# Reciprocal deviations of the tokens spread over channels through DRAM instead of by matmuls

## The reference, cut to what matters

```python
mu = jnp.mean(xs, axis=-1, keepdims=True)
var = jnp.mean((xs - mu) ** 2, axis=-1, keepdims=True)
xn = (xs - mu) / jnp.sqrt(var + EPS) * ln_g + ln_b
mid = jax.nn.silu(xn @ fc1_w + fc1_b) @ fc2_w + fc2_b
qkv = (xs @ qkv_w)...          # q, k normed by head, linear attention, o normed
o = o + mid
o = o @ proj_w + proj_b
```

## Time and profile before

| | |
|---|---|
| median of 3 runs | 2871.93 us (2860.03 to 2872.58) |
| the profiled execution's own time | 2866.76 us |
| its span | 2864.9 us |
| PE busy | 2757.2 us, 96% of the span |
| PE weight loads busy | 2522.9 us |
| DVE busy | 2035.1 us, 71% |
| ACT busy | 1184.9 us, 41% |
| POOL busy | 687.1 us, 24% |
| mean granted PE clock | 0.964 of full |

### The profile page before, as it was taken

One profiled execution on the slowest core, in us unless ns is written; L12 is line 12 of the kernel. 1 busy time (PEld: TensorE's weight loads), 2 busy tenths in 40 slices (PEclk: granted clock), 3 DMA queues, 4 the chain that ended last, 5 costly groups with the idle time before them and its releaser, 6 DMA issues.

```text
span 2864.9 us, 41194 instructions
## 1 busy us (share of the span) xinstructions
PE 2757.2 (96%) x14894; PEld 2522.9 (88%) x14894; DVE 2035.1 (71%) x2635; ACT 1184.9 (41%) x2043; POOL 687.1 (24%) x211
## 2 busy tenths in 40 slices
PE   6997799999999999999999999999999999999999
PEld 4555699899998899899998899999999899999998
DVE  5968784988887694988887693888887634444443
ACT  3431365444432366444442265444442254333332
POOL 0010052222224053322224053322224033211220
PEclk9998799999999999999999999999999999999999
DMA  5247642333236732333236733233326732111110
GB/s 218 61 120 236 218 126 76 96 96 96 97 117 212 254 123 89 96 96 96 96 104 212 264 115 99 76 107 100 102 96 196 270 97 68 39 39 47 41 39 30
DMA packets 189739, 341.14 MB, mean 119 GB/s; under 512 B 10720, under 2 KB 173152, under 8 KB 186720
## 3 DMA queue, kind: packets, MB, share of 16 engines
q1 hardware_dynamic: 180528, 311.59, 33.4%
q0 software_dynamic: 4480, 19.27, 2.3%
q10 hardware_dynamic: 4528, 7.57, 0.8%
HBM read 234.89 MB, written 103.51 MB: 118 GB/s over the span
## 4 chain that ended last, share of the span: by engine, by line
PE 77%; issue 9%; DVE 5%; DMA 5%; ACT 2%; POOL 1%; SPq 1%; DVEq 0%; ACTq 0%; POOLq 0%
PE bank L756 16%; PE bank L758 16%; PE bank L757 16%; PE bank L802 4%; PE bank L961 4%; PE bank L963 4%; PE bank L962 4%; PE bank L1161 3%; PE bank L983 3%; PE bank L1145 2%; DMA X<-x_scr 2%; DVE AC L2379 1%; PE bank L1112 1%; PE bank L1216 1%; PE bank L732 1%
## 5 line engine op out<-in xcount | busy, mean ns | idle before, releaser
L1728 ACT ACTIVATE S<-bank,b1p 128x448 f32<-128x448 f32 x336 | 212.8, 633 | 875.5 <-PE bank L758 873.8
L2379 DVE SCALAR_TENSOR_TENSOR AC<-XV,wfold,AC 128x1568 f32<-128x1568 f32 x288 | 530.4, 1847 | 2.8
L756 PE MATMUL bank<-SH,W2H 128*128 128x448 f32 x1008 | 393.2, 390 | 4.4 <-DVE SL L2348 4.4
L758 PE MATMUL bank<-SH,W2L 128*128 128x448 f32 x1008 | 377.9, 375 | 0.0
L757 PE MATMUL bank<-SL,W2H 128*128 128x448 f32 x1008 | 376.6, 374 | 0.0
L756 PE MATMUL bank<-XRH,W1H 128*128 128x448 f32 x1008 | 373.6, 371 | 0.0
L758 PE MATMUL bank<-XRH,W1L 128*128 128x448 f32 x1008 | 370.1, 367 | 0.0
L757 PE MATMUL bank<-XRL,W1H 128*128 128x448 f32 x1008 | 369.1, 366 | 0.0
L674 POOL TENSOR_TENSOR rq<-qn,nhalf 112x32 f32<-112x32 f32 x28 | 181.9, 6495 | 427.9 <-DVE qn L2318 427.9
L666 POOL TENSOR_TENSOR rk<-kn,nhalf 112x24 f32<-112x24 f32 (+1 forms) x56 | 200.8, 3598 | 285.8 <-DVE kn L2140 285.8
L678 POOL TENSOR_TENSOR ro<-on,nhalf 112x32 f32<-112x32 f32 x28 | 179.8, 6422 | 311.6 <-DVE on L2339 311.5
(11 more groups left out here) (237 smaller groups left out, 5375.4 us busy)
## 6 DMA issues: line engine op xcount, KB each, us to landing
X<-x_scr SPq DMA_DIRECT2D x52, 672.0 KB, 5.1
XV<-in_xp SPq DMA_DIRECT2D x36, 870.0 KB, 6.7
XC<-in_xp SPq DMA_DIRECT2D x14, 1682.0 KB, 11.9
CQ<-q_scr SPq DMA_DIRECT2D x28, 672.0 KB, 7.7
CX<-in_x SPq DMA_DIRECT2D x28, 672.0 KB, 4.9
x_scr<-CX SPq DMA_DIRECT2D x28, 672.0 KB, 5.7
V<-v_scr SPq DMA_DIRECT2D x28, 672.0 KB, 4.9
Y<-x_scr SPq DMA_DIRECT2D x28, 672.0 KB, 4.2
```

The lines of the kernel that those rows point to most:

```text
L756: mm(o, wh, xh, start=first, stop=False)
L758: return mm(o, wl, xh, start=False, stop=stop)
L1728: fn(S[:, j % 2, :], bank[j % 2][:, 0:T], ACT.Silu, bias=b1p[:, j:j + 1]).then_inc(s["s_s"], 1)
L2379: stt(o, XV[h][:, ky:ky + HR, kx:kx + W], wfold[:, kind, k, 3 * ky + kx:3 * ky + kx + 1], o, ALU.mult, ALU.add).then_inc(s["va"], 1)
```

## The change

The diagonal matrices, the 8 matmuls and the bank are taken out. ACT instead issues two DMAs for each tile: a write of rr (112 x 4) to a DRAM scratch of 448 numbers, and, once that write has landed, a read of these 448 numbers to each of the 128 partitions (RB). `scale_x` waits for the read and multiplies by RB. The waits of PE for `xsr`, and one for `oc_ev` ahead of the first tile's `spread_r`, go too.

```diff
@@ buffers
-        rh, rl = sb("rh", [TS, SUB], F32R, at=at), sb("rl", [TS, SUB], at=at)
-        DH, DL = sb("DH", [TS, SUB, TS], F32R, at=at), sb("DL", [TS, SUB, TS], F32R, at=at)
+        RB = sb("RB", [P, T], at=list(at))
+        at[0] += 2 * C * 4
-        o1r = sb("o1r", [TS, P], F32R, at=at)
+    r_d = scratch("r_scr", (SUB, TS))
@@ PE
-                def spread_r(n, p):
-
-                    pe.wait_ge(s["dg"], n * 2 + 2)
-                    for u in range(SUB):
-                        mm(bank[p][:, u * TS:(u + 1) * TS], o1r[:, :], DH[:, u, :], start=True, stop=False)
-                        last = mm(bank[p][:, u * TS:(u + 1) * TS], o1r[:, :], DL[:, u, :], start=False, stop=True)
-                    last.then_inc(s["rb_mm"], 1)
@@ PE, offset_dots
-                    pe.wait_ge(s["xsr"], n0 + 1)
@@ PE, last tile of the key and value stage
-                        if (t, u) == (STRIPS - 1, 3):
-                            if nxt:
-                                pe.wait_ge(s["oc_ev"], (b + 2) * (2 * KC))
-                            spread_r(n0, 7)
@@ PE, attend
-                    if u == 1:
-                        pe.wait_ge(s["xsr"], n + 1)
@@ PE, pre, step 4
                         pe.wait_ge(s["ml"], n * KC)
-                        spread_r(n, 6)
                         query_norms(n, 7)
@@ ACT
+                def roots_out(n):
+
+                    act.wait_ge(s["rr_s"], n + 1)
+                    act.dma_start(r_d.rearrange("u p -> p u"), rr[:, :], allow_slow_non_contiguous=True).then_inc(s["r_st"], 16)
+
+                def roots_spread(n):
+
+                    act.wait_ge(s["r_st"], n * 16 + 16)
+                    act.dma_start(RB[:, :], r_d.rearrange("(o u) p -> o (u p)", o=1).to_broadcast([P, T])).then_inc(s["r_ld"], 16)
@@ ACT, last tile of the key and value stage
+                        if (t, u) == (STRIPS - 1, 1):
+                            roots_out(n0)
                         values_out(n, t, u)
+                        if (t, u) == (STRIPS - 1, 2):
+                            roots_spread(n0)
@@ ACT, tile
                     silu(n, 6)
                     if not last:
+                        roots_out(n + 1)
                         query_out(n + 1, 1)
                         query_out(n + 1, 2)
+                        roots_spread(n + 1)
                     silu(n, 7)
@@ DVE (the call of token_diag is gone from both stages)
-            def token_diag(n):
...
-            def scale_x(n, p):
-                dve.wait_ge(s["rb_mm"], n + 1)
-                tt(X[:, :, :], X[:, :, :], bank[p][:, 0:T].unsqueeze(1).to_broadcast([P, KC, T]), ALU.mult).then_inc(s["xsr"], 1)
+            def scale_x(n):
+                dve.wait_ge(s["r_ld"], n * 16 + 16)
+                tt(X[:, :, :], X[:, :, :], RB[:, :].unsqueeze(1).to_broadcast([P, KC, T]), ALU.mult).then_inc(s["xsr"], 1)
```

More of the change, by code:

```diff
@@ L262, in build @@
             wo_ld kxs kxh kxl k_mm v_mm k_sq k_ev v_ev k_red k_rs k_hat v1_st0 v1_st1 at_mm ab_s
-            x_ld v_ld y_ld y_st xh xl xt_mm bn_s ag_s rve_s rr_s rh_s rl_s dg rb_mm xsr xrh xrl
+            x_ld v_ld y_ld y_st xh xl xt_mm bn_s ag_s rve_s rr_s r_st r_ld xsr xrh xrl
             q_mm q_ev qq qs_mm qn_s rq_s qa_mm o_sc o_mx o_sq o_red ro_s o_fin ot_mm
@@ L2218, in keys_values @@
                         key_scale(n - 1, 1 - t % 2, 1)
-                    if last:
-                        first_tile("diag")
                     if nxt:
@@ L2232, in keys_values @@
                             dve.wait_ge(s["ktp"], KTB + (b + 1) * (2 * KC))
-                        dve.memset(f(o1r[:, :]), 1.0)
                         for u in range(2):
@@ L2255, in run @@
                         token_var(n)
-                    elif what == "diag":
-                        token_diag(n)
                     elif what == "scale":
-                        scale_x(n, 7)
+                        scale_x(n)
                     elif what == "split":
@@ L2429, in tile @@
                     conv(t, 4)
-                    if not last:
-                        token_diag(n + 1)
                     split_s(n, 5)
@@ L2443, in tile @@
                     if not last:
-                        scale_x(n + 1, 6)
+                        scale_x(n + 1)
                         query_norm(n + 1, 7)
```

## The result

| | before | after |
|---|---|---|
| median | 2868.12 us (2858.72 to 2872.58, 6 runs) | 2842.23 us (2832.71 to 2849.12, 6 runs) |
| profiled execution, its own time | 2866.76 us | 2844.07 us |
| its span | 2864.9 us | 2842.3 us |
| mean granted PE clock | 0.964 | 0.966 |

The ratio is 0.9908, with a 95% interval from 0.9888 to 0.9928. The changed kernel is 25.9 us faster, where the forecast's terms gave 33.1 us (23.5 + 7.7 + 1.9).

What follows compares the result with a forecast made beforehand. PE, busy 96% of the span, was taken as the bound. 2866.76 - 23.5 (matmuls) - 7.7 (clock) - 1.9 (DVE) = 2833.7 us, plus 1 us towards the runs' mean: 2835 us, 8-in-10 range 2814 to 2858.

Steps and rivals of the forecast that it cites:

- The matmuls removed: Eight spread matmuls leave PE in each of 28 tiles, 0.84 us per tile, all on the path: -23.5 us.
- PE's clock: Less poorly filled time on PE around the norms: some 5 fewer clock falls of 1.54 us each, -7.7 us.
- the starting count: Before the change, 21 of 24 regular tiles' 8 us windows show a PE clock under 1.00, three show 1.00.
- DVE: DVE loses 1.48 us of work per tile; PE's waits for ML in images 0 to 2 go, -1.9 us.
- is worth nothing by itself: DVE's removed `token_diag` work, 41 us over 28 tiles, gains nothing by itself because DVE is not the bound.
- the rival of the taken gain: In images 0 to 2 PE's 0.84 us per regular tile goes to other waits, no clock gain: 2858 us, chance 0.10.
- The DMAs: ACT's write and read per tile, taken as 3 and 2 us, are covered by other work: 0 us.
- The cover of 5.6 us up to ACT and 6.7 us up to PE: Time from the write's issue to its landing beyond which ACT is late (5.6 us) and PE waits (6.7 us).
- the list of what would show me wrong: DVE or PE waiting for the DMA, the write landing after over 5 us, or falls moving the other way.
- The rival of the slow write: The 4-byte write lands late and holds ACT, then PE; at 10 us landing, 2913 us; chance 0.08.
- the estimate of 24 us for each us: Every us of write landing beyond PE's cover costs 24 us over the regular tiles.

Runs made afterwards that it cites:

- e12: Changed kernel, but DVE still does its four operations on the reciprocals, whose results nobody uses: 2846.31 us, ratio 0.9935.
- e2: Kernel before, with buffers rh and rl moved behind the others so that XRH, XRL and S lie 64 bytes lower: 2873.79 us, ratio 1.0016.
- e1: Changed kernel with 64 bytes left free behind rr, putting XRH and XRL back at their old addresses: 2837.39 us, ratio 0.9894.
- e3: Changed kernel with the scratch as 112 x 4, a contiguous write, and DVE reading RB with a stride: 2848.93 us, ratio 0.9928.
- e4: Changed kernel without its two DMAs, X multiplied by a constant -0.5 instead of the reciprocals: 2837.25 us, ratio 0.989.
- e5: Changed kernel with e1's padding and a contiguous write, PE turning every fourth token so RB is read as before: 2831.76 us, ratio 0.9876.
- e8: Changed kernel with RB read from 128 different rows of the input, reciprocals not applied: 2840.81 us, ratio 0.9909.
- e7: Changed kernel with only 8 of the 24 small query-norm matmuls per tile, so the norms are wrong: 2815.66 us, ratio 0.9822.
- e13: As e10, but the 24 norm matmuls stay together in the first tile of images 0 to 2: 2814.17 us, ratio 0.9830.
- e9: Changed kernel with the write issued and waited for twice: 3119.87 us, ratio 1.0883.
- e10: e5's kernel with the norm matmuls in two groups of 12, nine second-layer matmuls of block 6 between them: 2827.7 us, ratio 0.9853.

## Why the prediction was right, and where it was not

**The matmuls removed (-23.5 us): right.** The norms start 0.20 us after the W1L matmul. At equal time at the lower clock, a tile of the last image is 0.55 us shorter, and the other 0.29 us are in the W1 pitch. Over all runs, the clock-free time is 14.9 us lower, and the terms for matmuls and address give -23.5 + 8.2 = -15.3 us. In images 0 to 2 this gain needs DVE's relief beside it, as e12 shows.

**What was missing in the sum: the address of XRH.** The prediction costed the removed buffers at nothing, by not naming them. They moved the moving operand of 3024 matmuls by 64 bytes, 2.7 ns each, +8.2 us. e2 has this alone in the kernel before, where it costs 8.2 us clock-free. e1 takes it back in the changed kernel, and there the pitch returns but only 0.9 us clock-free (4.8 us by the medians) are gained. So the term is shown for the kernel before; what it costs the changed one beside the slow write is less, and how much is open.

**PE's clock (-7.7 us): the direction right, the size somewhat small, the starting count misread.** The 24 windows behind the earlier trace rows have 20 under 1.00 and four at 1.00, not 21 and three; 26% of 20 is still some 5. In the profiled execution the trace's clock records after 430 us add up to 124.3 us at the lower level before and 107.8 us after: 16.5 us less, worth half of that in time, -8.2 us. The windows under 1.00 went from 20 to 18, fewer than the 5 that were forecast. But one execution says little: in e1, e3, e4, e5, e8 and e12, whose norms are those of after, they number 13, 13, 12, 14, 16 and 11, and in e2, which still has the spread, 21. So it is 20 and 21 of 24 with the spread and 11 to 18, 14 on average, without: the shorter stretch does fall less often, by more than in proportion, and after's profiled execution lies at the upper end by chance. Over all runs the time lost to the lower level, (1 - mean clock) x span, is 102.1 us before and 90.4 us after, 11.7 us less, give or take 6. That the small matmuls bring the falls is shown by e7, where none of 24 is left, and by e13, where the 21 tiles with halved norms have none and the three with whole norms all fall (behind a wait of PE for ML as well). The Trainium skill (TensorE: Matmul & The Clock Gate, Part 1) has the clock released by recent activity; the trace agrees, in e9 most of all, with 0.50 to 0.53 in the windows behind waits of 7.2 us on average.

**DVE (-1.9 us): wrong.** The waits for ML did not go; they grew to 2.6 us. In the second tile of image 0, 0.60 us of DVE's 1.48 us turned into a wait for POOL, while PE came 0.84 us earlier. DVE's timeline there:

```profile
507.12 1.76 DVE L2328 TENSOR_TENSOR V<-V,ro 112x1536 f32<-112x1536 f32 x1 [0.60 <-POOL ro L678]
...
512.98 1.68 DVE L2337 TENSOR_TENSOR ML<-bank,MH 128x448 fp32r<-128x448 f32 x3
```

The sentence that DVE's relief "is worth nothing by itself" also failed. e12 puts it at some 8 us: without it PE's gain in images 0 to 2 would in part have become waits for DVE, as the rival of the taken gain has it. The point against that rival, that DVE gains more than PE, fits this.

**The DMAs (0 us): right in time, wrong in size.** I took 3 us for the write from the 224 KB stores, and it is 6.3 us; I took 2 us for the read, and it is 5.3 us. The cover of 5.6 us up to ACT and 6.7 us up to PE was worked out rightly, and it just held: ACT stands at the second DMA in front of S, PE has 0.7 us to spare in the tile shown, and e4 without DMAs has the same tiles in the last image and the same clock-free time. By the list of what would show me wrong, the landing over 5 us, DVE's wait for RB and ACT's wait of over 1 us all came, without a price here. It was close: the write lies on the chain that ended last in three tiles, and with the shorter pitch (e1 against e5) it went with some 9 us. That the term came out at nothing is in part luck. The rival of the slow write, given 0.08, was closer than that chance says. e9 shows its price: 278 us for waits of 174 us, so the estimate of 24 us for each us was too small, since the clock stays at its lower level behind such waits. The Trainium skill (DMA: Bandwidth & Descriptors, Rules for kernel authors) asks that a last dim which is not contiguous be rearranged. Here this is confirmed: 448 pieces of 4 bytes landed after 6.3 us, 112 pieces of 16 bytes after 1.6 to 1.7 us. Its fixed cost of about 2 us (Anatomy of one DMA, described there for transfers that GpSimd issues) is near the second and far under the first, where the measurement decides.

**The sum again**, for the profiled execution: -23.5 (matmuls) - 8.2 (clock) + 8.2 (address) - 0.9 (PE's waits from 430 us on, 37.0 to 36.1 us; 3.3 and 3.4 us of them have no releaser) = -24.4 us. Measured are 2866.76 - 2844.07 = 22.7 us. The remaining 1.7 us are not accounted for. Over all runs the sum is -11.7 (clock) - 14.9 (clock-free) = -26.6 us, and the medians differ by 25.9 us. So the forecast of 33.1 us was 7 us too large: the address (+8.2) was missing in it, DVE's 1.9 us at the waits for ML did not come, and the clock gave some 4 us more than was booked. The terms do not simply add, though: e12 shows that the gain on PE depends on DVE's relief, and e1 that the address, taken back alone, returned only part of its price.

## What to carry to other kernels

When a change removes or adds a buffer, list which operands move with it and look at the pitch of the matmuls that stream them: in e2, 64 bytes cost a third of what the change gained. A round trip through DRAM costs nothing only as long as it is shorter than the chain behind the waiting engine, so measure it in the form in which it will run: write contiguous pieces and arrange the order where the data is produced. Small matmuls in one stretch cost more than their own time where the clock falls behind them, and putting full-size ones between two halves avoids that, as long as PE has not just stood in front of the first half and no engine waits for the second.

## What the runs showed of the hardware that was not expected

- A 448-column matmul had a pitch of 200 ns with its moving operand at one address and 202.7 ns with it 64 bytes lower, in two kernels, with and without DMA traffic.
- A write of 448 separate 4-byte words to DRAM landed after 6.3 us, and a read of these words 5.3 us after its issue instead of 3.0 to 3.2 us. As 112 pieces of 16 bytes, the write landed after 1.6 to 1.7 us.
- A stride of 16 bytes on one operand raised DVE's float32 multiplication of 128 x 1344 from 1.55 to 2.58 us.
- Behind 24 small matmuls in 2.29 us the clock fell to 1.2 GHz in 11 to 18 of 24 tiles. With 8 of them it fell in none. With twice 12 and nine full-size matmuls between, it fell in none of the 21 tiles of e13 built that way and in three of the 24 of e10, those in which PE had waited 0.9 us in front of the first twelve.
